# Attention keys: four of the sixteen rotated key products of each tile computed on GpSimd, twelve on VectorE

## What is computed

```
qkv = x @ qkv_w.T + qkv_b          # 8 heads of 32
scores = einsum('bnhd,bmhd->bhnm', q, k) * scale
t = square(scores + C_SHIFT)       # in place of exp
attn = t / sum(t, axis=-1)
out = einsum('bhnm,bmhd->bnhd', attn, v)
```

## Time and profile before

| | us |
|---|---|
| median of the runs (3) | 4254.01 |
| lowest and highest run | 4253.61, 4260.93 |
| span of the profiled execution | 4333.9 |
| attention stage in it, about | 2130 to 3690 |
| DVE L1266 in it, 200 instructions | 455.9 |
| GpSimd busy in it, whole span | 1641.7 |

### The profile page before, as it was taken

One profiled execution on the slowest core, in us unless ns is written; L12 is line 12 of the kernel. 1 busy time (PEld: TensorE's weight loads), 2 busy tenths in 40 slices (PEclk: granted clock), 3 DMA queues, 4 the chain that ended last, 5 costly groups with the idle time before them and its releaser, 6 DMA issues. The chain is left out here.

```text
span 4333.9 us, 64637 instructions
## 1 busy us (share of the span) xinstructions
PE 3640.3 (84%) x24130; PEld 2345.7 (54%) x24130; DVE 2902.6 (67%) x2667; ACT 2306.3 (53%) x3514; POOL 1641.7 (38%) x734
## 2 busy tenths in 40 slices
PE   5779899898889989997688978888988889288787
PEld 1257777777777777776334342434333342256565
DVE  6258888888888888887767574767566673643311
ACT  1376667666667766663354637454654645342221
POOL 1257877777877777886000000000000000224422
PEclk9899999999999999999799999999999999588898
DMA  5500101110101110101201110111112010424433
GB/s 198 157 32 31 40 17 41 40 36 31 41 20 38 41 36 32 40 12 58 57 1 53 43 41 12 51 52 24 23 56 57 1 24 30 140 89 146 136 114 116
DMA packets 119427, 238.94 MB, mean 55 GB/s; under 512 B 22246, under 2 KB 83982, under 8 KB 116018
## 3 DMA queue, kind: packets, MB, share of 16 engines
q1 hardware_dynamic: 107266, 203.22, 15.0%
q0 software_dynamic: 11392, 31.02, 2.2%
q10 hardware_dynamic: 432, 0.20, 0.0%
HBM read 135.85 MB, written 79.27 MB: 50 GB/s over the span
## 5 line engine op out<-in xcount | busy, mean ns | idle before, releaser
L712 DVE TENSOR_TENSOR prod<-ps,win 128x1792 f32<-128x1792 f32 x630 | 1241.4, 2018 | 159.9 <-PE ps L783 116.1
L783 PE MATMUL ps<-ident,prod 128*128 128x128 f32 x8820 | 1093.6, 280 | 168.3 <-DVE prod L712 152.9
L783 PEld LDWEIGHTS ps<-ident,prod 128*128 128x128 f32 x8820 | 1027.6, 145 | 313.0 <-DVE prod L712 170.1
L1699 POOL DMA_DIRECT2D ident<-in_ident x1 | 0.6, 578 | 1627.7 <-POOLq L925 1627.7
L1168 ACT ACTIVATE phq<-ps 128x896 f32<-128x896 f32 x448 | 384.7, 918 | 201.0 <-PE ps L1431 200.1
L1266 DVE TENSOR_TENSOR phk<-kv 128x2048 f32<-128x2048 f32 (+1 forms) x200 | 455.9, 2282 | 1.2 <-issue 0.7
L468 POOL TENSOR_TENSOR y<-a1w,x2w 128x1568 f32<-128x1568 f32 x98 | 320.8, 3274 | 326.6 <-PE ps L763 308.3
L611 ACT ACTIVATE ps<-lg 128x448 f32<-128x448 f32 (+1 forms) x322 | 315.2, 982 | 239.9 <-DVE prod L712 239.9
L632 ACT ACTIVATE lg<-ps,par 128x392 f32<-128x392 f32 x392 | 390.9, 997 | 32.7 <-PE ps L770 31.3
L625 ACT ACTIVATE y<-ps,u2c,s2c 128x392 f32<-128x392 f32 x392 | 266.8, 681 | 223.9 <-PE ps L763 221.8
L762 PE MATMUL ps<-y,cw1bd 128*128 128x392 f32 x784 | 330.2, 503 | 36.2 <-ACT y L618 29.0
(11 more groups left out here) (264 smaller groups left out, 5314.3 us busy)
## 6 DMA issues: line engine op xcount, KB each, us to landing
win<-planes SPq DMA_DIRECT2D x14, 2480.0 KB, 8.7
qst<-qsp SPq DMA_DIRECT2D x96, 196.0 KB, 4.5
planes<-stage SPq DMA_DIRECT2D x7, 1984.0 KB, 7.0
xs<-in_x SPq DMA_DIRECT2D x8, 1568.0 KB, 21.3
conv_dram<-osb SPq DMA_DIRECT2D x14, 896.0 KB, 4.6
t<-in_x SPq DMA_DIRECT2D x28, 448.0 KB, 4.0
xn<-conv_dram SPq DMA_DIRECT2D x28, 448.0 KB, 6.9
t_dram<-tout SPq DMA_DIRECT2D x28, 448.0 KB, 2.9
```

The lines of the kernel that those rows point to most:

```text
L712: v.tensor_tensor(prod[b.buf(t)][:].rearrange("p (s h w) -> p s h w", h=RW, w=W), w, xw, ALU.mult).then_inc(prod_ready, 1)
L783: mm = pe.matmul(acc[:, at:at + P], x[:, at:at + P], ident[:], start=(t == 0 and k % 4 == 0), stop=(t == NU - 1), is_transpose=True, skip_ ...
```

## The change

GpSimd gets its own `keys`: in every tile it multiplies the last four rotations (13 to 16), 512 products per partition, into columns `FPOOL` to `FLIN` of `phk`. It waits for the same two things as VectorE's instruction (`wrapped` of tile j, `s_mm` of tile j - 2) and raises a new semaphore `phi_p`. VectorE's instruction shrinks from sixteen rotations to twelve, 1536 products. TensorE waits for `phi_p` too before `S(j)`. The semaphore `out_gate2` is dropped and its one increment goes to `gate2`; nothing waits for either.

```diff
+ROTP = 4
+FPOOL = (ROT - ROTP) * DH
...
+        phi_p = sem("phi_p")
...
+            def keys(b, hg):
+                for j in range(NT):
+                    n = b * HG * NT + hg * NT + j
+                    r = tile_rows(j)
+                    pool.wait_ge(wrapped, n + 1)
+                    if j >= 2:
+                        pool.wait_ge(s_mm, n - 1)
+                    ki = kv[j % 3][0:r, 0:HPG * KX].rearrange("p (h i) -> p h i", i=KX)[:, :, 0:DH]
+                    kr = bass.AP(ki.tensor, ki.offset + ROT - ROTP, [ki.ap[0], ki.ap[1], [1, ROTP], [1, DH]])
+                    pool.tensor_tensor(phk[j % 2][0:r, :, FPOOL:FLIN].rearrange("p h (r i) -> p h r i", i=DH),
+                                       ki.unsqueeze(2).broadcast_to([r, HPG, ROTP, DH]), kr, ALU.mult).then_inc(phi_p, 1)
+
+            with pool.Fori(0, B) as b:
+                for hg in range(HG):
+                    keys(b, hg)
...
-                sp.sem_inc(out_gate, 1)
+                sp.sem_inc(gate, 1)
...
-                    kr = bass.AP(ki.tensor, ki.offset + 1, [ki.ap[0], ki.ap[1], [1, ROT - 1], [1, DH]])
-                    v.tensor_tensor(phk[j % 2][0:r, :, DH:FLIN].rearrange("p h (r i) -> p h r i", i=DH),
-                                    ki.unsqueeze(2).broadcast_to([r, HPG, ROT - 1, DH]), kr, ALU.mult).then_inc(phi, 1)
+                    kr = bass.AP(ki.tensor, ki.offset + 1, [ki.ap[0], ki.ap[1], [1, ROT - 1 - ROTP], [1, DH]])
+                    v.tensor_tensor(phk[j % 2][0:r, :, DH:FPOOL].rearrange("p h (r i) -> p h r i", i=DH),
+                                    ki.unsqueeze(2).broadcast_to([r, HPG, ROT - 1 - ROTP, DH]), kr, ALU.mult).then_inc(phi, 1)
...
                     pe.wait_ge(klin, 2 * (n + 1))
                     pe.wait_ge(phi, n + 1)
+                    pe.wait_ge(phi_p, n + 1)
```

More of the change, by code:

```diff
@@ L975, in attention_stage @@
         gate = sem("gate2")
-        out_gate = sem("out_gate2")
         x_in = [sem(f"x_in2{c}") for c in range(NCT)]
```

## The result

The changed kernel takes 4295.32 us (median of 4 runs, 4291.96 to 4297.78) against 4255.41 (4 runs) for the kernel before: a ratio of 1.0091, interval 1.0079 to 1.0103. It is 39.9 us slower. The forecast was 4289 us, 35 more.

What follows compares the result with a forecast made beforehand. VectorE and TensorE were both taken as nearly the bound of a pass. With the two products taking turns, a pass takes 67.05 us against 62.71, +35 over eight: 4254 + 35 = 4289 us, range 4252 to 4325.

Steps and rivals of the forecast that it cites:

- That the two exclude each other: In each tile, VectorE's product with two SBUF inputs and GpSimd's SBUF-reading product wait for each other's whole instruction.
- VectorE's product, D = 1.75: VectorE's product of 1536 instead of 2048 elements takes 1.75 us on its own, saving 0.53 a tile.
- GpSimd's product, P = 1.25: GpSimd's product of 512 elements, two SBUF inputs, takes 1.25 us on its own, with ends 0.96 and 1.42.
- The handover, -0.31: Where VectorE's and GpSimd's products take turns, a little overlap is given back: 0.31 us off a round.
- Hard exclusion: Rival: no overlap at the handover, 3.00 us a tile, 4349 us; chance 0.12 above 4323, together with a slow GpSimd.
- The round, 2.69: One product on each engine per tile: D + P - 0.31 = 1.75 + 1.25 - 0.31 = 2.69 us.
- The order: In a round GpSimd's product comes first, while VectorE evacuates the next tile, then VectorE's product; 0.8 us of slack.
- A pass, 67.05: A pass of 25 tiles takes 67.05 us against 62.71, +4.3 a pass, +35 us over eight.
- That the difference goes to the end in full and no further: What follows a pass waits for its last `S`, so the passes' +35 us reaches the kernel time in full.
- the clock falls: Rival: TensorE, busy 86% of a round, drops to half clock, its 2.30 us becoming 4.6; chance 0.02 for a whole pass.
- What the profile would show: VectorE's product some 2.5 us long, GpSimd's some 2.2, its first near 1.25; TensorE waiting for VectorE in nearly every tile.
- no exclusion: Rival: the two products overlap, TensorE's 2.30 us a tile decides, 48 us less, 4206 us; chance 0.05.

## Why the prediction was right

*That the two exclude each other*: right, and shown from four sides. Taken away at VectorE's input or at GpSimd's reads, the loss turns into a gain of 1.5%; put into the kernel before with no shared data, it costs 2.5%; enlarged, it costs 3%.

*VectorE's product, D = 1.75*: measured 1.748.

*GpSimd's product, P = 1.25*: measured 1.19, within the ends 0.96 and 1.42. That it came so near has some luck in it, as two errors met: 1.75 to 1.88 ns an element was too little (1.92 to 1.99), and 0.32 us fixed too much (0.2).

*The handover, -0.31*: measured 1.75 + 1.19 - 2.67 = 0.27. VectorE ends 0.13 less than D after GpSimd, as in the earlier trace rows; GpSimd's side is 0.13 too (2321.12 less 1.19 is 2319.93, against VectorE's 2320.06), where the rows of before gave 0.15 to 0.21. Hard exclusion, a round of D + P = 2.94, is refuted.

*The round, 2.69*: 2.67, again with luck. By the sum of the prediction P alone would have made the eight passes 12 us too long (0.06 x 25 x 8), and the handover alone some 8 us too short (0.04 x 24 x 8). *The order* was as told: GpSimd's first, the record of VectorE's starts 0.13 after its last one ended. *A pass, 67.05*: 66.53. The second pass was taken for all eight; the mean of the eight is 63.2 before and 67.1 now, and they grew by 31.5 us where 35 was forecast.

*That the difference goes to the end in full and no further*: this step was a little off, in the other direction. The stage grew by 6.1 us more than the passes. Some 3 of them lie between the last product and `gram`: that gap was 1.40 to 1.42 us in six of eight passes before, and 2.4 in the two others; now it is 2.4 in five. In the longer ones TensorE runs at half its clock. At the end of the second pass of the changed kernel, against before, `S` of the last tile:

```profile
2381.63 2.15 PE L1429 MATMUL ps<-phk,kv 64*32 64x288 f32 x16 [0.52 <-issue]
```

```profile
2374.54 1.18 PE L1409 MATMUL ps<-phk,kv 64*32 64x288 f32 x16 [0.91 <-issue]
```

```profile
2381.00:2384.00 3.00, 2.38 (x32) 1.11 (x24) 0.58 (x2) 0.05 (x1) 0.00 (x0) 0.50 1.05 389
```

The granted clock of that stretch is 0.50, so 1.2 GHz, and 1.18 us of matmuls become 2.15. In the tiles before, TensorE was busy 42.24 of 49.00 us where it had been 44.74, at full clock in both. Whether that is why the clock falls earlier was not tested. The other runs don't settle it: the gap is 1.41 us in all eight passes with VectorE's factor in PSUM, with GpSimd writing alone and with the copied keys, in four with one rotation on GpSimd, and in two with eight.

The other 3 us of the stage lie between the passes too, behind `gram`. From a pass's last product to the first of the next it is 924.3 us in sum over the seven, 917.3 before, and 4 of these 7 are the gaps. The largest growth is behind the second pass (3.8 us) and the third (2.2), and there the mean granted clock of the 20 us behind the last product is 0.56 and 0.83, where it had been 0.83 and 0.96. So the rival "the clock falls" was present with some 3 us, and perhaps 6, at the ends of the passes and between them, and not for a whole pass. The 2.3 us outside the stage I didn't trace; the interval of the ratio is 5 us to either side.

So 35 was 39.9: some 3 less from a cheaper round, 3 more from the clock at the ends of the passes, 3 more between the passes where the clock is the likely cause, and 2.3 not assigned.

*What the profile would show*: the records of 2.55 and 2.21 us and the shortest GpSimd product near P were as told. The wait list was not: it books TensorE's wait under "issue".

*The rival "no exclusion"*, 2.30 a tile and 48 us less, was priced too low where the runs brought it about. The kernel with the keys in PSUM gains 1.6%, 69 us. Its tile is TensorE's 2.24 instead of 2.54, 0.30 less, 60 us; and at the end of each pass, where two products stood back to back for 4.48 us, the shorter product counts in full. The eight passes sum to 442.7 us, 62.9 less than before. The gap behind them is 1.41 in all eight, 2 us less, and the last 4 I didn't trace.

## What to carry to other kernels

Before giving a part of VectorE's work to GpSimd, look where the inputs of VectorE's instructions lie: if both are in SBUF and GpSimd reads SBUF, the two run one after the other. Where they take turns all the time, as here, the sum to write down for a round is D + P less some 0.27 us, not the larger of the two; it held for 2.67, 3.07 and 3.15 us. Where another engine's loop is longer than that round, as TensorE's with one rotation, that loop sets the pace. One input in PSUM, put there by an engine with time to spare, made the same division 1.6% faster than the kernel before instead of 0.9% slower. An instruction whose median duration is far over its shortest at one shape is where to look for this, since busy time includes the wait.

## What the runs showed of the hardware

- GpSimd's product of two SBUF inputs at 512 elements took 1.19 us reading `kv`, and 1.06 at the shortest reading `bk_s` in the same shape. What makes the difference was not tested.
- The kernel before took 4255.41 us in one session and 4343.57 and 4340.80 in others, with passes of 505.6 us in its own trace and 507.7 in that of its variant with the PSUM factor. No trace of it is at 4255. The changed kernel's trace, of a run of 4291.96 us, has 569.4 us for the last stage, the nine other traces have 650.8 to 661.2, so the difference most likely lies there; its cause is open.
